# Mixture-of-experts decoder layer: a 128-row slice runs its gate, up, transposes and down in turn, without the next slice's first gate-up unit inside it

## What is computed

```python
shared = jax.nn.silu(x @ Ws_gate) * (x @ Ws_up) @ Ws_down
scores = jax.nn.softmax(x @ W_router, axis=-1)
topk_vals, topk_idx = jax.lax.top_k(scores, TOP_K)        # 2 of 8 experts
h = jax.nn.silu(jnp.einsum('td,edh->eth', xf, We_gate)) * jnp.einsum('td,edh->eth', xf, We_up)
y_all = jnp.einsum('eth,ehd->etd', h, We_down)            # hidden width 352
routed = jnp.einsum('etd,te->td', y_all, combine)
```

## Time and profile before

| | |
|---|---|
| median of 3 runs | 1088.21 us |
| profiled execution, its own time | 1088.47 us |
| span of the profile | 1086.8 us |
| PE busy | 1016.1 us (93%) |
| PE weight loads busy | 858.2 us (79%) |
| VectorE (DVE) busy | 666.1 us (61%) |
| ScalarE (ACT) busy | 456.7 us (42%) |
| GpSimd (POOL) busy | 275.8 us (25%) |
| mean granted PE clock | 0.974 of full speed |

### The profile page before, as it was taken

How to read it: one execution, slowest core, us unless ns; L and a number is a source line. 1 busy time by engine, 2 the same in 40 slices (tenths; PEclk the granted TensorE clock), 3 DMA queues, 4 the chain that set the end, 5 groups by cost and what they waited for, 6 DMA issues and landing times. The chain is left out here.

```text
span 1086.8 us, 18081 instructions
## 1 busy us (share of the span) xinstructions
PE 1016.1 (93%) x6368; PEld 858.2 (79%) x6368; DVE 666.1 (61%) x1502; ACT 456.7 (42%) x798; POOL 275.8 (25%) x367
## 2 busy tenths in 40 slices
PE   7899999999979999999859979999999999899997
PEld 5688888888778888887637768888998889778785
DVE  4836556477265776776444847776777776253576
ACT  5623314145125544454443226555655664221110
POOL 4510100213143323333343122212231220503040
PEclk9999999999978999999998979999999999999999
DMA  5403032023877888884432157787778773615042
GB/s 168 180 1 116 0 115 87 0 81 126 205 187 194 212 228 239 218 219 131 171 99 81 63 179 225 252 256 266 243 246 277 251 244 113 213 40 188 6 155 77
DMA packets 87183, 172.66 MB, mean 159 GB/s; under 512 B 8112, under 2 KB 36016, under 8 KB 85328
## 3 DMA queue, kind: packets, MB, share of 16 engines
q1 hardware_dynamic: 81008, 150.08, 44.6%
q0 software_dynamic: 6112, 21.76, 6.1%
HBM read 130.92 MB, written 37.49 MB: 155 GB/s over the span
## 5 line engine op out<-in xcount | busy, mean ns | idle before, releaser
L45 PE MATMUL e_ps_h<-e_x_lo,e_gu_hi 128*128 128x256 f32 (+1 forms) x384 | 111.3, 290 | 10.8 <-DVE e_x_lo L2141 8.7
L45 PE MATMUL a_ps_proj<-region_a_rounded,arena 128*128 128x512 f32 x272 | 107.4, 395 | 11.2 <-DVE region_a_rounded L369 6.2
L953 DVE CUSTOM_DVE_ANT_0 b_dump<-b_ps_s,b_mask 128x128 f32<-128x128 f32 (+1 forms) x256 | 80.4, 354 | 46.5 <-PE b_ps_s L1143 43.3
L47 PE MATMUL e_ps_h<-e_x_hi,e_gu_hi 128*128 128x256 f32 (+1 forms) x384 | 108.2, 282 | 0.0
L46 PE MATMUL e_ps_h<-e_x_hi,e_gu_lo 128*128 128x256 f32 (+1 forms) x384 | 108.2, 282 | 0.0
L46 PE MATMUL a_ps_proj<-region_a_rounded,arena 128*128 128x512 f32 x272 | 106.4, 391 | 0.0
L47 PE MATMUL a_ps_proj<-region_a_rounded,arena 128*128 128x512 f32 x272 | 106.4, 391 | 0.0
L2147 DVE TENSOR_TENSOR e_gu_lo<-f_region_a,e_gu_hi 128x704 fp32r<-128x704 f32 x92 | 81.3, 889 | 26.8 <-ACT e_gu_hi L2057 26.3
L388 DVE SCALAR_TENSOR_TENSOR f_region_b<-a_ps_proj,a_taps,f_region_b 128x510 f32<-128x510 f32 (+2 forms) x96 | 71.7, 746 | 40.8 <-ACT f_region_b L328 38.5
L843 ACT ACTIVATE b_pt<-b_ps_x 128x384 f32<-128x384 f32 x128 | 61.8, 487 | 61.2 <-PE b_ps_x L1167 61.1
L757 POOL TENSOR_SCALAR_AFFINE_SELECT b_pt<-b_pt 128x256 f32<-128x256 f32 x128 | 51.8, 407 | 122.6 <-ACT b_pt L843 121.9
(11 more groups left out here) (400 smaller groups left out, 2693.7 us busy)
## 6 DMA issues: line engine op xcount, KB each, us to landing
f_region_a<-we_gate_up SPq DMA_DIRECT2D x88, 352.0 KB, 5.6
qk_split<-arena SPq DMA_DIRECT2D x24, 512.0 KB, 5.8
y_slots<-f_region_b SPq DMA_DIRECT2D x16, 512.0 KB, 3.4
f_x_next<-x SPq DMA_DIRECT2D x7, 1024.0 KB, 7.1
b_sk<-qk_split SPq DMA_DIRECT2D x24, 256.0 KB, 4.4
b_sq<-qk_split SPq DMA_DIRECT2D x24, 256.0 KB, 5.7
f_region_a<-we_down SPq DMA_DIRECT2D x12, 512.0 KB, 4.0
f_region_b<-we_down SPq DMA_DIRECT2D x11, 512.0 KB, 4.0
```

The lines of the kernel that those rows point to most:

```text
L45: pe.matmul(out, a_hi, b_lo, start=first, stop=False)
L47: return pe.matmul(out, a_hi, b_hi, start=False, stop=last)
L953: ins = dve.tensor_tensor_reduce(dump[:, n % 2, cols], ps_s[:, n % 2, cols], mask[:, cols], -1.0, 3e38, ALU.add, ALU.min, peak[:, u, k, i: ...
```

## The change

On the tensor engine the small tile loses both sides of the next tile's unit 0: it runs gate, up, the next tile's transposes of tokens, its own three transposes, and down. Every large tile, those behind a small one too, begins with its own unit 0. The wait for `silu_done` in front of the early gate side goes with it, as does the one early unit ahead of the loop. In the lists of ScalarE and VectorE, `split_x` of the next tile goes from the middle of the small tile to behind the rounding and subtraction of the turned product, and on VectorE `split_down` goes from behind the product `small_hf` to ahead of it. The number of instructions that compute is the same.

```diff
@@ scalar, small_tile
                 act.activation(small_sg, bank(0), ACT.Silu).then_inc(silu_done, 1)
-                split_x(m, k + 1)
                 act.wait_ge(h_ready, U * number(m, k) + 3)
                 last = E_UNITS[2]
                 act.activation(small_hi[:, 0:2], ps_t[:, 0:2], ACT.Copy)
                 act.activation(small_hi[0:last, 2], ps_t[0:last, 2], ACT.Copy).then_inc(h_hi_done, 1)
+                split_x(m, k + 1)
@@ vector, small_tile
                 split_gate_up(m, k + 1, 3)
-                split_x(m, k + 1)
+                split_down(m, k)
                 dve.wait_ge(silu_done, count(m, k, U, 1) + 1)
                 dve.wait_ge(h_ready, U * number(m, k) + 2)
                 dve.tensor_tensor(small_hf[:], bank(1), small_sg, ALU.mult).then_inc(h_done, 1)
-                split_down(m, k)
...
                     .then_inc(h_lo_done, 1)
+                split_x(m, k + 1)
                 output(m, k)
@@ tensor, large_tile
+                hidden(m, k, 0)
                 if k % SPAN == 1:
-                    hidden(m, k, 0)
                     turn(m, k + 1)
@@ tensor, small_tile
                 small_hidden(m, k, 0)
+                small_hidden(m, k, 1)
                 turn(m, k + 1)
-                small_hidden(m, k, 1)
-                pe.wait_ge(silu_done, count(m, k, U, 1) + 1)
-                hidden(m, k + 1, 0, (0,))
                 small_turn(m, k)
-                hidden(m, k + 1, 0, (1,))
                 small_down(m, k)
@@ tensor, ahead of the loop
             turn(0, 0)
-            hidden(0, 0, 0)
             with pe.Fori(0, TURNS) as m:
```

## The result

The changed kernel takes **1122.34 us**, the median of 4 runs (1117.44 to 1125.91), against 1087.11 us for the kernel before (4 runs): a ratio of 1.0317, with a 95% interval of 1.0285 to 1.0349. It is 35 us slower; forecast were 1124 us and a range of 1109 to 1133.

What follows compares the result with a forecast made beforehand. TensorE was taken to set the experts' pace, so added waits lengthen the run. Chain 18.0, `h_lo` wait 4.6 and clock 13.2 us sum to 35.8 us, giving 1124 us against the median, range 1109 to 1133 us.

Steps and rivals of the forecast that it cites:

- the cover: Small tile: PE's work on the next tile's unit 0 hides silu, product, rounding and subtraction; the change removes it.
- the two places named: Small tile: PE waits before the three transposes, 3.0 us in the first, and before the down products, 1.3 us.
- The chain: Small tile, chunk 3's subtraction to the next large tile's unit 1: 9.80 us instead of 7.23, 18.0 us for seven.
- The wait for `h_lo`: Large tile behind a small one: ScalarE and VectorE start unit 0 later, 0.65 us more, 4.6 us for seven.
- The clock: Small tiles: PE's idle time drops the clock to half in six of seven, 2.2 us each, 13.2 us.
- the two places behind this term: Trace of before, at 638.3 and 927.9: PE waits around transposes, then half clock for 10.2 and 3.35 us.
- The page on transposes: Small tiles: by the skill's rule transposes don't count as PE activity; all seven fall, 15.4 us, 1126 us in all.
- What was to cost nothing: `split_x` behind the chain, gathers, SP's queue, the early unit ahead of the loop, the dropped `silu_done` wait: 0 each.
- The loads that catch up: ScalarE's 12.1 us of waits for gate-up chunks shrink as DMA gets early: at most 12 us, 1112 us; chance 0.12.
- The loads as the pace of the stage: Weight loads, not PE, pace the experts, so PE's new idle time replaces chunk waits: 1088 us; chance 0.03.
- The spells of 7 us: Half clock lasts 7 us in each small tile, as after 640.5: 22 us, 1133 us in all; chance 0.07.
- The clock that holds: The clock stays full in most small tiles, leaving chain and `h_lo` wait: 1111 us; chance 0.18.

Runs made afterwards that it cites:

- Experiment 5: Changed kernel with `dn_lo` back behind `small_hf` on VectorE and ScalarE ordered silu, chunk 3, down weights: 1099.7 us, 1.0105 of the kernel before.
- experiment 6: Changed kernel, next tile's chunk 0 split ahead of unit 0's work in large tiles behind small ones: 1119.9 us; with PE's idle time also filled with products, 1108.8 us.
- experiment 1: Changed kernel with PE's two idle times per small tile filled with 11 and 8 extra products, results unread: 1109.5 us, 1.0196 of the kernel before.
- Experiment 2: Changed kernel with PE's two idle times per small tile filled with 18 and 12 transposes of 128x128: 1111.6 us, 1.0219 of the kernel before.
- the repeat: The changed kernel measured once more, unaltered: 1122.3 us, 1.0326 of the kernel before.
- experiment 3: Changed kernel with VectorE's subtraction for `dn_lo` moved back behind the product `small_hf`: 1104.5 us, 1.0163 of the kernel before.
- experiment 6's first run: Changed kernel, next tile's chunk 0 split ahead of unit 0's work in large tiles behind small ones, idle time not filled: 1119.9 us, 1.0309 of the kernel before.
- experiment 6's run with the idle time filled: Changed kernel with chunk 0 split ahead of unit 0's work and extra products in PE's two idle times: 1108.8 us, 1.0183 of the kernel before.

## Why the prediction was right, and where not

- **That the cover was what counted**: right. In its own order PE waits at the two places named, 2.4 and 1.38 us in the first small tile (I had 3.0 and 1.3), seven times each. Chunk 3's subtraction came 4.2 us into that tile and not 4.8, which explains the first figure. The other waits before the transposes were 1.75 to 3.25 us (I had 1.4 to 3.6). Experiment 5 shows that 1.9 us per tile stay with all the lists that were tried.
- **The chain, 2.57 us per tile, 18.0 us**: measured 2.74, 19.2 us. The steps were 3.05 for 3.07 at the transposes, 4.97 for 4.85 at down. Those 0.12 us are 0.05 more from the transposes to the rounding (685.72 to 686.30, 0.58 for 0.53) and 0.09 more from the end of the last subtraction to PE's start (687.50 to 687.64, 0.14 for 0.05), less the 0.02; the other 0.05 are spread over the products.
- **The wait for `h_lo`, 0.65 us, 4.6 us**: measured 0.58, 4.1 us. Taking tile 0, which was already in the new order, as the pattern held; experiment 6 confirms the cause.
- **The clock, 13.2 us**: right in kind, too large in size. Six of seven tiles fell as forecast, but the step "5 us of products, midway between 3.35 and 7.0" was mis-sized: the spells last 3.4 us in five tiles and 6.8 in one, and cost 1.3 to 2.0 us each, 9.3 us in all (experiment 1: 8.4 us of stage). The mean of the stretch was 0.96 and not 0.93. One of the two places behind this term was misread, too: the clock fell at 640.5, and the wait of 2.06 us that I counted ahead of that fall ended at 643.73, behind it. What PE did before 640.5 was one wait and the start of 8 transposes, so only the place at 927.9 showed two waits before a fall. In the trace of before:

```profile
640.10 1.57 PE L2233 MATMUL e_ps_x<-f_ident,f_region_b 128*128 128x128 f32 x8 [1.83 <-PEq L1441]
```

- **The page on transposes**: I weighed the rule of the Trainium skill ("TensorE: Matmul & The Clock Gate", Part 4) that transposes don't count as activity, and took the fall at 930.6 as agreeing. Experiment 2 shows the other way in seven tiles, so here the measurement decides. At that place, too, the waits of 1.70 and 1.42 us can be enough: in the repeat, 1.72 and 1.38 us with three transposes between them brought a fall. The forecast of six falls did not hang on it.
- **What was to cost nothing** cost nothing: `split_x` behind the chain, SP, the gathers, the dropped wait for the silu. No new wait for them is in the profile.
- **Rivals.** The loads that catch up: ScalarE's waits for gate-up chunks went from 12.1 to 10.9 us, and chunk 3 starts 0.19 us sooner; a tenth of what that rival needed. The loads as the pace of the stage: PE's new idle time did come on top, and the DMA engines are at 0.65 instead of 0.73, no. The spells of 7 us: one of six. The clock that holds: only in one tile of seven here, but in six of seven once the subtraction is moved back (experiment 3), so it was close.
- **The sum**: 35.8 forecast, 35.2 measured between the medians. That it came within 1 us is luck: of the terms, 18.0, 4.6 and 13.2 us were forecast, and 19.2, 4.1 and 9.3 measured, with 1.3 off for chunk 3. The expert part itself grew by 32.2 us (31.4 in the repeat), and the 3 us up to the medians are within the scatter of the runs.

## What to carry to other kernels

When work of a later step stands between the parts of a serial chain through three engines, cost its removal by the chain and not by the moved instructions: measure from the last event that both orders share, add each engine's own duration and the hand-overs, which were 0.03 to 0.14 us here, and put every instruction that stands ahead of a link in its engine's list into the sum. Then look at where in a list the long, patient pieces stand: one subtraction of 1.75 us, ahead of instead of behind a product of 0.52 us, made half of this change's loss (and cost 6.4 us in the order with the cover), and putting first what TensorE needs first made a kernel that is faster than either. Two idle times of 1.2 to 3.3 us close together brought a spell of half clock in 19 of 21 small tiles (the changed kernel, its repeat and experiment 6's first run), and in one of seven when the first of them was cut to 1.5 us or less (experiment 3), so an edit that shortens them can pay twice.

## What the runs showed of the hardware that I had not expected

Transposes keep TensorE's clock up. With 18 and 12 of them in the idle times, 2.13 and 1.47 us long, the granted clock was 1.00 from 666 to 944 us; with those times idle it was 0.96 over the same part. That is shown for these fp32 transposes of 128x128 and this kernel.

Whether a fall comes is not settled by the sum of a tile's two idle times: in experiment 3, 1.28 + 1.74 us brought one in the second small tile, 1.48 + 1.74 us none in the first; in the changed kernel 1.75 + 1.38 us brought none, and in its repeat 1.72 + 1.38 us did:

```profile
882.69 0.55 PE L2268 MATMUL e_ps_t<-f_ident,e_small_hf 128*128 128x128 f32 x3 [1.72 <-DVE e_small_hf L2194]
885.40:888.75 3.35, 3.35 (x11) 2.77 (x10) 0.75 (x2) 0.00 (x0) 0.00 (x0) 0.50 0.86 278
```

Nor is it settled by the longest of them. In experiment 6's run with the idle time filled, PE stood still for 3.44 us before the transposes of the first small tile, and the clock stayed full:

```profile
687.17 0.55 PE L2274 MATMUL e_ps_t<-f_ident,e_small_hf 128*128 128x128 f32 x3 [3.44 <-DVE e_small_hf L2200]
680.00:690.00 10.00, 6.46 (x41) 5.77 (x40) 7.04 (x10) 6.55 (x11) 3.10 (x4) 1.00 0.75 254
```

What does settle it stays open. How long a spell lasted went with when it began. In the 20 small tiles with a fall where nothing was filled (the changed kernel, its repeat, experiment 3 and experiment 6's first run), the 12 spells that began behind the start of the down products, or at most 0.43 us ahead of it, lasted 3.4 us, and the 8 that began 0.84 to 2.97 us ahead of it lasted 6.8.
